# Expert weights split into halves during the first three images and kept in device memory

## What is computed

```python
x = conv_block(x)                  # group norm, q/k/v products, attention over 1024 points, residual
t = to_tokens(x)                   # 4 x 1024 tokens of 256
t = t + attention(layernorm(t))    # q, k, v through residual MLPs with SiLU, softmax over the queries
x_norm = layernorm(t)
probs = softmax(x_norm @ gate_w)                 # 8 experts
dispatch_w, expert_idx = top_k(probs, 2)
for e in range(8):
    h = gelu(x_norm @ w1[e] + b1[e])             # 256 -> 1024
    y = h @ w2[e] + b2[e]                        # 1024 -> 256
    out = out + combine[:, e:e + 1] * y
t = t + out
```

## Time and profile before

| | |
|---|---|
| median of 3 runs | 1202.08 us (1198.8 to 1202.88) |
| the profiled execution | 1199.52 us |
| its span | 1197.8 us |
| images | 0 to about 704 us |
| expert steps | about 704 to 1165 us |
| last rows, turned and stored | to 1197.8 us |
| PE busy | 1136.8 us, 95% |
| DVE busy | 774.6 us, 65% |
| ACT busy | 554.0 us, 46% |

### The profile page before, as it was taken

One profiled execution on the slowest core, in us unless ns is written; L12 is line 12 of the kernel. 1 busy time (PEld: TensorE's weight loads), 2 busy tenths in 40 slices (PEclk: granted clock), 3 DMA queues, 4 the chain that ended last, 5 costly groups with the idle time before them and its releaser, 6 DMA issues. The chain is left out here.

```text
span 1197.8 us, 24646 instructions
## 1 busy us (share of the span) xinstructions
PE 1136.8 (95%) x8066; PEld 1056.7 (88%) x8067; DVE 774.6 (65%) x1862; ACT 554.0 (46%) x1002; POOL 255.3 (21%) x311
## 2 busy tenths in 40 slices
PE   6999999999999999999999988998999999999993
PEld 5898898988998988998989878998999999999983
DVE  5676376785476775576864589676787668675751
ACT  3433354533344533345433457775775445454531
POOL 3010000100231100321100413236332323232320
PEclk9999999999999999999999999999999999999996
DMA  5001000110010110101000451358664354435328
GB/s 172 1 1 36 1 1 1 37 36 1 25 52 2 36 36 1 43 33 36 1 1 1 141 183 38 49 150 260 180 167 122 56 127 118 114 62 123 56 42 285
DMA packets 70630, 84.64 MB, mean 71 GB/s; under 512 B 11664, under 2 KB 62096, under 8 KB 70544
## 3 DMA queue, kind: packets, MB, share of 16 engines
q1 hardware_dynamic: 57104, 66.22, 17.6%
q0 software_dynamic: 13440, 17.32, 8.0%
HBM read 55.31 MB, written 29.25 MB: 71 GB/s over the span
## 5 line engine op out<-in xcount | busy, mean ns | idle before, releaser
L1686 PE MATMUL ps<-w2s,hs 128*128 128x256 f32 x1728 | 252.4, 281 | 16.1 <-DVE hs L1650 14.8
L1686 PE MATMUL ps<-xt,w1s 128*128 128x256 f32 x1746 | 256.7, 283 | 2.8 <-issue 2.8
L1686 PEld LDWEIGHTS ps<-w2s,hs 128*128 128x128 f32 x1728 | 223.0, 189 | 22.0 <-DVE hs L1650 11.7
L1686 PEld LDWEIGHTS ps<-xt,w1s 128*128 128x128 f32 x1746 | 225.5, 189 | 3.5 <-issue 3.5
L1030 ACT ACTIVATE h<-ps,b1t 128x256 f32<-128x256 f32 x288 | 137.2, 478 | 126.5 <-PE ps L1686 80.1
L764 POOL DMA_INDIRECT acc_rows<-y_w,now_s x72 | 119.2, 1656 | 171.0 <-ACT y_w L1048 93.5
L1648 DVE CAST hs<-h 128x256 fp32r<-128x256 f32 x288 | 88.2, 306 | 96.5 <-ACT h L1030 55.2
L1650 DVE TENSOR_TENSOR hs<-h,hs 128x256 fp32r<-128x256 f32 x288 | 123.6, 429 | 9.9
L1686 PE MATMUL ps<-xs,wh 128*128 128x512 f32 x384 | 121.4, 397 | 1.5 <-issue 1.4
L1686 PEld LDWEIGHTS ps<-vk,pr 128*128 128x128 f32 x768 | 94.6, 188 | 6.8 <-DVE pr L1504 3.0
L1686 PE MATMUL ps<-vk,pr 128*128 128x256 f32 x768 | 96.4, 280 | 3.2 <-DVE pr L1504 2.0
(11 more groups left out here) (235 smaller groups left out, 1716.4 us busy)
## 6 DMA issues: line engine op xcount, KB each, us to landing
w1r<-in_w SPq DMA_DIRECT2D x13, 1024.0 KB
w2r<-in_w SPq DMA_DIRECT2D x13, 1024.0 KB
xg<-sorted_rows SPq DMA_DIRECT2D x38, 272.0 KB
b2t<-in_b SPq DMA_DIRECT2D x37, 128.0 KB
xn<-in_x SPq DMA_DIRECT2D x4, 1024.0 KB, 5.0
acc_rows<-r_out SPq DMA_DIRECT2D x4, 1024.0 KB, 4.8
rows<-acc_rows SPq DMA_DIRECT2D x8, 512.0 KB, 7.3
out_tokens<-cols_out SPq DMA_DIRECT2D x8, 512.0 KB, 8.5
```

What stands on the lines that cost most here:

```text
L1686: ins = t.matmul(out, left[l], right[r], start=first and n == 0, stop=last and n == 2, **more)
```

## The change

The split is done once for all eight experts, in the images 0, 1 and 2, and kept in device memory in `weight_halves` (8 experts × 2 matrices × 128 × 2 halves × 2048). There are 64 pieces of 128 × 512. SP loads a piece (256 KB) into one of four places of `piece`, ACT writes its high half (`piece_hi`), DVE the low half over the raw one (`piece_lo`), SP stores both (512 KB). Images 0, 1 and 2 do 16 pieces in the second attention (`MANY_AT`), images 1 and 2 another 8 in the first (`FEW_AT`). `piece` lies over the second pair of `us`, so DVE waits for the stores before it writes there. The experts load both halves (2 MiB per matrix) straight to where the products read them, and `w_piece`, `ws_act`, `ws_dve` and the branches of ACT and DVE go.

```diff
+        FEW, MANY = 8, 16
+        FEW_AT = {2: (0, 1), 3: (2,), 5: (3, 4), 6: (5, 6), 7: (7,)}
+        MANY_AT = {0: (0, 1), 1: (2, 3), 2: (4, 5), 3: (6, 7), 4: (8, 9), 5: (10, 11), 6: (12, 13, 14), 7: (15,)}
...
+            def piece_out(e, j, made):
+                w, c, k = j // 4 % 2, j % 4, j % 4
+                sp.wait_ge(p_lo, made)
+                sp.sem_inc(sp_held, 1)
+                sp.dma_start(halves_d[bass.ds(e, 1), w, :, :, c * HALF:(c + 1) * HALF]
+                             .rearrange("e p h f -> (e p) h f"), piece[:, k, :, :].bitcast(F32)).then_inc(p_out[k], 16)
+
+            AHEAD = 2
...
+            def pieces(e, count, b, many):
+
+                for j in range(many):
+                    piece_out(e + j // 8, j, count(b, j + 1))
+                    if j + AHEAD < many:
+                        landed = count(b, 16 * ((j + AHEAD) // 4), 4)
+                        piece_in(e + (j + AHEAD) // 8, j + AHEAD,
+                                 None if isinstance(landed, int) and landed == 0 else landed)
...
             image(0, True, False)
+            many_pieces(0)
             with sp.Fori(1, B - 1) as b:
+                first_pieces_in(b * 3 - 1, before_few, b)
                 rows_of(b - 1)
+                few_pieces(b)
                 image(b, False, False)
+                many_pieces(b)
             rows_of(B - 2)
...
             def load_weights(s, n, u):
 
-                sp.wait_ge(ws_act, at(s, 8, -8))
-                sp.sem_inc(sp_held, 1)
-                sp.wait_ge(ws_dve, at(s, 8, -8))
+                sp.wait_ge(h_mm, at(s, FC, -FC))
                 sp.sem_inc(sp_held, 1)
                 with sp.If(sp.value_load(fresh[0:1, bass.ds(s, 1)], min_val=0, max_val=1) == 1):
-                    weights(n, expert(s))
+                    first_weights(n, expert(s))
+                    sp.wait_ge(y_mm, at(s, FC, -FC))
+                    sp.sem_inc(sp_held, 1)
+                    second_weights(n, expert(s))
...
-            weights(0, expert(0))
-            biases(0, expert(0))
+            for k in range(4):
+                sp.wait_ge(p_out[k], before_few(B - 1, 0, 4))
+            for n in range(2):
+                first_weights(n, expert(n))
+                second_weights(n, expert(n))
+                biases(n, expert(n))
             sp.wait_ge(rows_free, B)
             gather(0, 0, True)
             gather(1, 1, True)
-            weights(1, expert(1))
-            biases(1, expert(1))
...
-                    load_weights(s + 2, n, i + 1)
...
                     gather(s + 2, n, False)
                     if not (unrolled and s == 0):
                         load_biases(s + 1, 1 - n)
+                    load_weights(s + 2, n, i + 1)
...
+            def piece_hi(j, landed):
+
+                k = j % 4
+                act.wait_ge(p_in[k], landed)
+                a.copy(piece[:, k, 0, :], piece[:, k, 1, :].bitcast(F32)).then_inc(p_hi, 1)
...
+            def piece_lo(j, made):
+
+                k = j % 4
+                dve.wait_ge(p_hi, made)
+                v.tensor_tensor(piece[:, k, 1, :], piece[:, k, 1, :].bitcast(F32), piece[:, k, 0, :].bitcast(F32),
+                                ALU.subtract).then_inc(p_lo, 1)
...
                 if f == 0:
-                    pe.wait_ge(ws_dve, at(s, 8, 4))
+                    pe.wait_ge(w1_in[n % 2], at(i + n // 2, 16, 16))
...
-                if f % 2 == 0:
-                    pe.wait_ge(ws_dve, at(s, 8, 5 + f // 2))
+                if f == 0:
+                    pe.wait_ge(w2_in[n], at(i, 16, 16))
```

More of the change, by code:

```diff
@@ new lines, in piece_out, with first_pieces_in @@
+            def piece_out(e, j, made):
+                w, c, k = j // 4 % 2, j % 4, j % 4
+                sp.wait_ge(p_lo, made)
[3 more added lines that the diff above has]
+            AHEAD = 2
+            def first_pieces_in(e, count, b):
+                for j in range(AHEAD):
+                    landed = count(b, 0, 4)
+                    piece_in(e, j, None if isinstance(landed, int) and landed == 0 else landed)
@@ L906, in image @@
                         normal(b - 1, i - 3)
+                    if not first and not last:
+                        for j in FEW_AT.get(i, ()):
+                            piece_hi(j, before_few(b, 16 * (j // 4) + 16, 4))
                     if i + 2 < NT:
@@ L955, in image @@
                         norm_hi(b + 1, i - 2)
[L956 to L969 removed]
+                    if not last:
+                        for j in MANY_AT.get(i, ()):
+                            piece_hi(j, before_many(b, 16 * (j // 4) + 16, 4))
             for k in range(KC):
@@ L1443, in image @@
                         max1(i + 2)
+                    if not first and not last:
+                        for j in FEW_AT.get(i, ()):
+                            piece_lo(j, before_few(b, j + 1))
                     if not first and i == 0:
@@ L1467, in image @@
                         dst = us[o % 2]
+                        if not first and o == 1 and n_u == R_PIECES:
+                            for k in range(4):
+                                dve.wait_ge(p_out[k], before_many(b, 0, 4) if not last else before_few(b, 0, 4))
                         step(v.tensor_copy(dst[0][:, m, c], prob[:, n_u % 2, 0:HALF]))
@@ L1529, in image @@
                         lo2(i)
+                    if not last:
+                        for j in MANY_AT.get(i, ()):
+                            piece_lo(j, before_many(b, j + 1))
                     if i + 2 < NT:
```

115 lines of the change are left out of this document (48 added, 67 removed).

## The result

The changed kernel takes 1277.03 us (median of 4 runs, 1275.02 to 1280.26) where the kernel before takes 1200.44 (4 runs): 1.0636 times as long, 95% interval 1.0605 to 1.0667. The forecast was slower, 1219 with a range from 1194 to 1242. The direction is right and the size far too small. The profiled executions are 1275.02 against 1199.52 us, 75.5 apart; the sum had said 17.

What follows compares the result with a forecast made beforehand. TensorE (PE), busy 95% of the span, was taken as the bound, so only its waits count. −18 + 24 (second attention) + 4.5 + 3 + 3.5 = +17 us gave a median of 1219, range 1194 to 1242.

Steps and rivals of the forecast that it cites:

- (a): Expert steps 12 to 35: pieces and branches go, a gain of 8.5 us, bounds 6.4 and 8.9.
- (b): Expert steps 0 to 11: PE's waits for DVE's low half go, a gain of 8 us, bounds 4 and 10.
- The step that failed in the experts: Experts outside the first loads and steps 8 to 10: weight loads hidden, next gather not delayed, costing nothing.
- such a pile only for steps 8 to 10: Three new experts in a row, some 18 MB in 40 us: a cost of 3.5 us, bounds −4 and 10.
- one long stop in turn 6: Second attention, images 0 to 2: three pieces ahead of exp(7) make PE stand 5.3 us, once per image.
- one at the end of the first attention: Images 1 and 2: two pieces stand before DVE's half for mix1(7), 2.3 us twice, 4.5 us; bounds 2.7 and 8.
- I take 2.7: Second attention, turns 1 to 5: round trip 6.7 us against a 5.55 us cycle, up to 5.7 an image, 2.7 taken.
- The 3 us for the first gather: Start of the experts: first loads, 8 MiB ahead of step 0's gather, delay it by 3 us, bounds 0 and 6.
- DMA becomes the bound: Rival: piece traffic loads the image stage, steps 8 to 10 starve, PE may be granted less; about 1244 us, chance 0.12.
- Pieces are covered: Rival: landing takes half, round trip fits the attention cycle, experts cost nothing or gain; 1192 us (1186 to 1198), chance 0.22.
- That the experts gain little: Caveat on experts: DVE's hidden tiles, not the pieces, are late; would lift every case by some 8 us.
- The loop's steps still uneven at new experts, now on a weight load: Sign in the expert loop that would show the prediction wrong; steps of 11.6 us would show it right.

Runs made afterwards that it cites:

- the loads halved: Changed kernel with every reload of an expert's weights bringing the high halves alone, 1 MiB per matrix instead of 2, same queue order: 1244.66 us, ratio 1.0371.
- engines alone: Changed kernel with ACT and DVE doing 64 copies and subtractions on an operand staying in SBUF, no piece transfers, split left out of the computation: 1223.82 us, ratio 1.0186.
- transfers alone: Changed kernel with SP loading each piece and storing raw values twice, ACT and DVE doing nothing for pieces, split left out: 1228.66 us, ratio 1.0203.
- three ahead with two in turn 6: Changed kernel with b1 loaded ahead of the weights, three pieces loaded ahead instead of two, and piece 14 moved from turn 6 to 7: 1217.28 us, ratio 1.0149.

## Why the prediction was wrong in size

Between the sum's 17 and the measured 75.5 are 58.5 us: 36 of them lie in the experts (−13.0 expected, +22.8 measured) and 24 in the images (28.6 expected, 52.7 measured); the rest is below 2 us, of the other sign.

**Bound, and terms (a), (b).** The reading of the earlier trace rows was right. Term (a), 8.5 us in steps 12 to 35, was there: with the loads halved these steps take 279.0 us for 287.8, 8.8 less. Term (b), 8 us, was 4.8 by the same run. In the changed kernel both stretches have the other sign, +15.7 and +7.1.

**The step that failed in the experts** is the sentence "Elsewhere, one expert's 4 MiB has a whole step per half, 11.6 us for 2 MiB: hidden", with "the next gather, queued behind, is needed a step later: nothing". Asking only when the weights were due was the mistake. They are due a step later, and PE hardly waits for them: in the steps no wait for either matrix is listed, and "issue" comes to 1.7 us. What mattered was what else is on that queue and on those 16 engines and is due earlier. The biases of the next step are issued a few us ahead of their use. In one reload of the changed kernel, SP and then ACT:

```profile
1123.80 0.33 SPq L586 DMA_DIRECT2D w1p<-weight_halves  x1
1127.61 0.33 SPq L590 DMA_DIRECT2D w2p<-weight_halves  x1
1129.21 0.39 SPq L611 DMA_DIRECT2D xg<-sorted_rows  x1
1130.71 0.34 SPq L600 DMA_DIRECT2D b1t<-in_b  x1
1131.23 0.33 SPq L602 DMA_DIRECT2D b2t<-in_b  x1
```

```profile
1141.02 1.21 ACT L1087 ACTIVATE h<-ps,b1t 128x256 f32<-128x256 f32 x3 [6.95 <-DMA b2t<-in_b]
```

```profile
1124.00:1138.00 14.00, 14.00 (x122) 14.00 (x122) 7.04 (x18) 4.49 (x10) 3.70 (x4) 1.00 1.00 346
```

The engines are full for 14 us at 346 GB/s, 4.8 MB, where a step has 11.62 us, and the bias comes 9.8 us after its issue. The prediction had worked out such a pile only for steps 8 to 10 and taken 3.5 us, of bounds −4 and 10; steps 8 to 11 took 9.7 more. It also had the figure for the answer, 8.39 MB at 350 GB/s in 24 us, and so 12 us for 4.19 MB, and used it for the first loads alone. The steps around a reload, 12 to 16 us in the loop and 16 to 20 in steps 8 to 10, cost 36.4 us against the halved loads, with the clock behind the waits in it.

**The step that failed in attention** is a size. The mechanism (round trip, ACT in its order, one long stop in turn 6, one at the end of the first attention) is what the traces show: engines alone and transfers alone cost 4.4 and 5.4 us, and one more piece ahead gives 31. Turn 6 was 4.4 to 5.8 for 5.3, the first attention 3.0 for 2.3. In turn 6 two errors met: the landing was about 1 us shorter than taken, which gives the 4.4 of image 0, and in image 1 piece 12 was late itself (ACT's copy at 379.14, so that DVE made it 0.9 us later than the sum had it), which the sum left out. Too small were "I take 2.7" for turns 1 to 5, with 4 to 5 us measured, and a term that is missing, the clock, 14.6 us:

| | predicted | measured |
|---|---|---|
| image 0 | 8 | 13.6: 9.1 idle, of which 4.4 in turn 6, and 3.9 busy at the lower clock |
| image 1 | 10.3 | 20.0: 13.7 idle, 6.3 clock |
| image 2 | 10.3 | 19.1: 14.6 idle, 4.4 clock |
| image 3 to first step | 1.5 | 1.1 (the wait for the gather 2.99, as taken) |
| steps 0–11 | −4.5 | +7.1 (−2.7 in 0 to 7, +9.7 in 8 to 11) |
| steps 12–35 | −8.5 | +15.7 |

(Idle and clock are of the windows above, whose ends are whole microseconds.) The 3 us for the first gather came out by another way than the sum's, whose run from 676 for 24 us also ends at 700 and not at 702: SP issues the gather when POOL's last row stores have landed, and beside the 8 MiB (373 GB/s from 732 to 756) that was 10.4 us after their issue (739.65 to 750.08) instead of 3.2 (689.01 to 692.25). The prediction does speak of a PE "granted less" after a wait, with the 0.90 of the earlier trace rows, but only in a rival and only as a remark. The size could have been bounded from matmuls at either level; as it was, the sum priced a wait at its own length.

**The rivals.** "DMA becomes the bound" (1244) was nearest: it named both things that happened, the experts starving for transfers and PE's lower clock, but only at steps 8 to 10 and at the first loads. Its 1244 is still 33 below the measured time. "Pieces are covered" was right about one thing, that the engines have the room for the work; three ahead with two in turn 6 brings image 0 to within 0.8 us. "That the experts gain little" was answered as the prediction had it: the pieces were DVE's trouble.

Of the signs to look for, ACT waiting at its copies and the one stop of 5 us were seen. "The loop's steps still uneven at new experts, now on a weight load" was the right warning, with another load.

**A correction to the description of the kernel before.** It says that in the 12 steps written out the pieces are split whether or not the expert changes. That holds for ACT alone (80 copies per matrix, 160 in all, are 20 × 8); DVE's 52 per matrix, 104 in all, are 13 × 8, one for each load. No term was worked out from it.

**Still open:** why `b2t` on a queue of its own is as late as behind the weights; and what sets how long the clock stays low after a stop, which differs between executions of the same images (14.6 and 20 us in all).

## What to carry to other kernels

Before a load is called hidden, list every other transfer that is issued while it runs, and when each is due: here the small one that was due first paid for the large one that was due late; a second queue did not save it, an earlier issue or a smaller load did. Work that waits for a transfer on an engine with an in-order program cost here neither the work nor the transfer but their round trip, and depth (one more piece in flight, 31 us) was worth more than moving work about (10 us). And a new wait of some microseconds on PE is priced with the slower matmuls behind it.

## What was not expected of the hardware

A transfer of 128 KB, issued from another engine's queue into full DMA engines, landed 11 us later (902.94 to 914.01), against the 3.5 to 3.9 us of a load of 256 KB behind a store in the second attention of image 0, where the engines' share was 0.70 (150 to 200). And 288 GB/s of piece traffic for 43 us of image 0 cost PE nothing (43.00 us busy of 43.00, at a granted clock of 1.00).
